# A recurrent recommendation kernel: the first 14 slots in another order, and the attention weights prepared in another way

## What is computed

```python
hs = _gru(hist, gru_W, gru_U, gru_b)
emb = jnp.concatenate([hs, news_b - hs, news_b, hs * news_b], axis=-1)
a = jax.nn.relu(jnp.einsum('bti,ij->btj', emb, att_W1) + att_b1)
a = jax.nn.relu(jnp.einsum('bti,ij->btj', a, att_W2) + att_b2)
ats = jax.nn.sigmoid(jnp.einsum('bti,ij->btj', a, att_W3) + att_b3)
...
def au_step(h, xs):
    xu_t, xr_t, xc_t, at_t = xs
    u = jax.nn.sigmoid(xu_t + h @ au_Uu)
    r = jax.nn.sigmoid(xr_t + h @ au_Ur)
    c = jnp.tanh(xc_t + r * (h @ au_Uc))
    u_ = at_t * u
    hn = (1.0 - u_) * h + u_ * c
    return (hn, None)
```

## Time and profile before

| | us |
|---|---|
| median of 3 runs | 1975.37 |
| lowest and highest | 1975.0, 1975.86 |
| the profiled execution | 1972.17 |
| its span, first to last instruction | 1970.3 |

### The profile page before, as it was taken

One profiled execution on the slowest core, in us unless ns is written; L12 is line 12 of the kernel. 1 busy time (PEld: TensorE's weight loads), 2 busy tenths in 40 slices (PEclk: granted clock), 3 DMA queues, 4 the chain that ended last, 5 costly groups with the idle time before them and its releaser, 6 DMA issues. The chain is left out here.

```text
span 1970.3 us, 29728 instructions
## 1 busy us (share of the span) xinstructions
PE 1934.8 (98%) x9190; PEld 861.8 (44%) x9190; DVE 1497.8 (76%) x2357; ACT 1452.0 (74%) x2466; POOL 1630.9 (83%) x1389
## 2 busy tenths in 40 slices
PE   8899999999999999999999999999999999999988
PEld 3344444444444444444444444444444444444433
DVE  5777777777777777777777777777777777777875
ACT  6677777777777777777777777777777777777754
POOL 6688888888888888888888888888888888888862
PEclk9999999999999999999999999999999999999999
DMA  3111111111111111111111111111111111111010
GB/s 122 54 44 71 49 48 66 51 51 50 70 48 48 70 48 53 48 70 48 48 70 50 51 48 69 48 48 70 53 48 48 69 48 50 69 52 48 33 44 22
DMA packets 37577, 108.15 MB, mean 55 GB/s; under 512 B 4329, under 2 KB 4585, under 8 KB 31153
## 3 DMA queue, kind: packets, MB, share of 16 engines
q1 hardware_dynamic: 37410, 107.60, 14.8%
q10 hardware_dynamic: 144, 0.26, 0.1%
HBM read 107.43 MB, written 0.42 MB: 55 GB/s over the span
## 5 line engine op out<-in xcount | busy, mean ns | idle before, releaser
L933 PE MATMUL ps<-h_hi,w_hi 128*128 128x512 f16 x1384 | 525.7, 380 | 19.7 <-DVE g L713 15.9
L934 PE MATMUL ps<-h_lo,w_hi 128*128 128x512 f16 x1384 | 524.8, 379 | 0.0
L935 PE MATMUL ps<-h_hi,w_lo 128*128 128x512 f16 x1384 | 524.8, 379 | 0.0
L306 POOL TENSOR_TENSOR hn_lo<-hn,hn_hi 128x512 f16<-128x512 f32 x200 | 232.4, 1162 | 182.2 <-ACT hn_hi L420 182.2
L300 POOL TENSOR_TENSOR hn<-h,news 128x512 f32<-128x512 f32 x200 | 256.1, 1281 | 74.1 <-DVE h L839 73.9
L566 ACT ACTIVATE ps<-gt,p_rest 128x512 f32<-128x512 f32 x196 | 135.3, 690 | 216.8 <-DVE gt L836 216.8
L370 POOL TENSOR_TENSOR gus<-gu,score 128x512 f32<-128x512 f32 x197 | 250.8, 1273 | 5.4 <-ACT gu L581 4.4
L319 POOL TENSOR_TENSOR x_lo<-x,x_hi 128x512 f16<-128x512 f32 x198 | 229.3, 1158 | 22.7 <-ACT x_hi L440 18.4
L363 POOL TENSOR_TENSOR g_lo<-g,g_hi 128x512 f16<-128x512 f32 x196 | 227.6, 1161 | 21.2 <-ACT g_hi L591 17.5
L827 DVE TENSOR_TENSOR gt<-gr,ps 128x512 f32<-128x512 f32 x196 | 135.0, 689 | 140.3 <-ACT gr L594 140.3
L377 POOL TENSOR_TENSOR d<-h,hc 128x512 f32<-128x512 f32 x186 | 236.7, 1273 | 0.4 <-ACT hc L587 0.4
(11 more groups left out here) (135 smaller groups left out, 3724.0 us busy)
## 6 DMA issues: line engine op xcount, KB each, us to landing
score<-score_rows SPq DMA_DIRECT2D x50, 1024.0 KB, 4.5
x<-in_xs SPq DMA_DIRECT2D x199, 256.0 KB, 3.0
news<-in_xs SPq DMA_DIRECT2D x4, 256.0 KB, 5.2
score_rows<-s_rows SPq DMA_DIRECT2D x50, 8.0 KB
p_rest<-in_pack_rest SPq DMA_DIRECT2D x1, 776.0 KB, 6.9
p_att<-in_pack_att SPq DMA_DIRECT2D x1, 322.0 KB, 5.4
x<-in_xs ACTq DMA_DIRECT2D x1, 256.0 KB, 4.0
p_gru<-in_pack_gru SPq DMA_DIRECT2D x1, 195.0 KB, 4.2
```

Source lines behind the costliest of these rows:

```text
L306: g.tensor_tensor(hn_lo[:, k, :], hn[:, k, :], hn_hi[:, k, :], ALU.subtract).then_inc(hnlo_ready, 1)
L933: m.matmul(ps[:, bank, :], w_hi[:, w, :], hi, start=start, stop=False)
L934: m.matmul(ps[:, bank, :], w_hi[:, w, :], lo, start=False, stop=False)
L935: return m.matmul(ps[:, bank, :], w_lo[:, w, :], hi, start=False, stop=stop)
```

## The change

- **Weights.** The pack of attention weights no longer holds the row of w3, and W1a, W1d and W2 stand side by side in it. W1a - W1b is written in place; the copy of W1d and both products with |w3| are gone, and one split of 320 columns takes the place of one of 384. |w3| is now the scale of the second layer's ReLU on ScalarE (an operand of one value a partition), and b2 is still multiplied by it.
- **Entry.** On VectorE the preparation is cut into parts that stand between the first states; the small ones (`prepare_att_2`) and the low parts of x of items 4 and 5, which GpSimd made before, stand ahead of the first attention sum. On ScalarE hn_hi(0), x_hi(4) and the c_news parts change places.
- **Slot 4.** On ScalarE hn_hi(3) goes behind the tanh and the sigmoid of the slot.
- **Slots 5, 9 and 13.** The first half of `attention_2` waits for two items less of a1_lo.
- **Slots 8 and 9.** The first score product goes from the end of slot 8 into its middle, and its sigmoid from the end of slot 8 to the place behind hn_hi of that slot.
- **Slots 10 to 13.** On TensorE the candidate product comes ahead of z, and the gated candidate input product (GXH) goes to the end. On VectorE step and state of g follow the difference at once. The splits of the gated weights stand one slot earlier.

```diff
-    SPLIT_X, SPLIT_G = LAG - 2, LAG + 2
+    SPLIT_X, SPLIT_G = LAG - 3, LAG + 1
...
             def early(low):
-                if low + 2 >= NC:
+                if low + 2 >= NC + 2:
+                    if low == NC:
+                        pool.wait_ge(xlo_ready, NC + 2)
                     input_low(low + 2, low + 3)
...
+            state_news_high(0, 1)
             reset_first(3)
             candidate_first(2)
-            second_high(0)
-            state_news_high(0, 1)
             state_high(1, 2)
             update_first(3)
+            second_high(0)
             candidate_first(3)
             act.wait_ge(att_landed, 16)
-            news_part(0)
             state_high(2, 3)
             state_news_high(1, 2)
+            news_part(0)
             news_part(1)
             second_high(1)
+            news_part(2)
             relu_1_high(0, 1)
-            news_part(2)
...
-                a.activation(ps[:, B_PAIR[p], :], ps[:, B_PAIR[p], :], ACT.Relu, bias=b_att2[:, 0:1]).then_inc(a2p_ready[p], NC)
+                a.activation(ps[:, B_PAIR[p], :], ps[:, B_PAIR[p], :], ACT.Relu, bias=b_att2[:, 0:1],
+                             scale=w3_col[:, 3:4]).then_inc(a2p_ready[p], NC)
...
-                if score_of(low - 1):
-                    score_rows_of(scored(low - 1), None)
                 if pairs_of(low - 1):
+                    if low - 1 == TILED:
+                        act.wait_ge(prep, 8)
...
                     news_part(3)
-                    act.wait_ge(a1_pe, 2)
-                    state_news_high(3, 4)
                     relu_1_high(1, 2)
                 else:
                     state_news_high(low - 1, low)
+                    if low == FIRST_SCORED:
+                        score_rows_of(NC, None)
                     relu_1_high(low - 2, low - 1)
...
                 if low == NC:
+                    act.wait_ge(a1_pe, 2)
+                    state_news_high(3, 4)
                     relu_1_high(2, 3)
...
                 if has(low - LAG - 1):
                     gated_difference(low - LAG - 1, low - LAG)
+                    gated_step(low - LAG - 1, low - LAG)
+                    gated_state(low - LAG - 1, low - LAG)
...
-                if has(low - LAG - 1):
-                    gated_step(low - LAG - 1, low - LAG)
                 attention_1_low(item, item + 1)
-                if has(low - LAG - 1):
-                    gated_state(low - LAG - 1, low - LAG)
...
             new_state_first(0)
-            prepare_att_terms()
-            prepare_att_blocks()
+            prepare_att_1()
             candidate_first(2)
             new_state_first(1)
-            split_att()
+            split_att_high()
             candidate_first(3)
             new_state_first(2)
+            split_att_low()
             new_state_first(3)
+            input_low(NC)
+            prepare_att_2()
+            input_low(NC + 1)
...
+                if low == FIRST_SCORED:
+                    pe.wait_ge(r_ready, low + 1)
+                    scores(NC)
                 if has(low - LAG):
-                    if low == LAG:
-                        pe.wait_ge(a1lo_ready, 2 * NC - 1)
-                    else:
-                        pe.wait_ge(g_ready, low - LAG)
-                    split_product(B_GXH, GW_C, *hg, start=True, stop=True).then_inc(gxh_pe, 1)
+                    candidate_part()
                     pe.wait_ge(gu_ready, low - LAG + 1)
...
-                pe.wait_ge(t1_ready, low + 1)
-                candidate_state(low - NC + 1, low - NC + 2)
-                if score_of(low):
+                if has(low - LAG):
+                    if low == LAG:
+                        pe.wait_ge(a1lo_ready, 2 * NC - 1)
+                    else:
+                        pe.wait_ge(g_ready, low - LAG)
+                    split_product(B_GXH, GW_C, *hg, start=True, stop=True).then_inc(gxh_pe, 1)
+                else:
+                    candidate_part()
+                if low > FIRST_SCORED and score_of(low):
+                    pe.wait_ge(r_ready, low + 1)
                     scores(scored(low))
                 if pairs_of(low):
-                    pe.wait_ge(a1lo_ready, low - 1)
+                    pe.wait_ge(a1lo_ready, low - 3)
                     pe.wait_ge(t2_ready, low + 1)
                     attention_2(0)
+                    pe.wait_ge(a1lo_ready, low - 1)
```

71 lines of the change are left out of this document (41 added, 30 removed).

## The result

The changed kernel takes 1956.47 us (median of 4 runs, 1956.07 to 1956.91) where the kernel before, run beside it, takes 1975.18 us (median of 4, 1971.69 to 1975.86). The ratio is 0.9907, with a 95% interval of 0.9895 to 0.9919. The forecast was 1958.9 us, so the kernel is faster, as said, and by 2.4 us more than the working gave. The profiled execution took 1956.07 us, 1954.2 us of it span; before it was 1972.17 and 1970.3 us. From profile to profile the span is 16.1 us shorter; the sum of the working was 16.5 us.

A forecast was written before the change was run, and what follows sets the result against it. TensorE was taken to bound the loop, leaving gains only in the first 115 us, at most 23.5 us. Terms summed to 16.5 us, taken off the 1975.37 us median: 1958.9 us, range 1954.5 to 1963.5 us.

The forecast's parts named there:

- Entry, +3.2 us: Kernel start: attention starts at 19.10 instead of 22.33 us, 3.2 us won, with a new 1.5 us wait.
- Slots 4 and 5, +2.4: Slot 5's candidate product loses its 1.88 us wait for t, 32.06 instead of 37.70 us: 2.4 us more won.
- the held instructions, -2.4: Small VectorE preparations before the first attention sum are held by GpSimd: 2.4 us lost, bounds 0 and 2.9.
- Rival (a): No holding on VectorE: 2.4 us more gained, 1956.4 us; chance 0.2.
- (b): All three VectorE instructions held, plus one more TensorE drop to 1.2 GHz (1.7 us): 1961.0 us; chance 0.25.
- (c): VectorE's instruction ring slower, 1 to 2 us a slot back in slots 11 to 14: 1963 to 1965 us; chance 0.08.
- (d): ReLU with a scale from memory much longer in 50 pairs; 1996.4 us at 1.0 us more each; chance 0.01.
- No slow stretch, +2.35: Slots 6 to 8 begin 8.0 us earlier without a 1.7 us slow stretch behind slot 5's wait: 2.35 us more won.
- The score, +2.6: Score sigmoid inside slot 8: the 2.66 us wait at slot 9's head shrinks to 0.3; 2.6 us won.
- slots 9 and 10, -0.65: Slot 9's second a1_lo comes some 0.7 us late and slot 10 loses 0.1: 0.65 us lost.
- Slots 11 to 13, +10.1: Waits for g (9.1 us) and a slow stretch (1.6) go, less 0.9 of new waits: 10.1 us won.
- Slot 14, -1.1: ScalarE starts slot 14 1.5 us further behind, making r late for the GR product: 1.1 us lost, once.

The follow-up runs named there:

- the kernel with nothing held ahead of the first sum: Changed kernel with the abs(w3) and b2 products in one-tensor-operand form, the w3 pair on ScalarE, x_lo(5) behind the first attention sum; 1954.28 us, ratio 0.9889.
- the kernel cut in three: Changed kernel with small preparations split: signs stay, products behind a1_lo(0), w3 pair in slot 5, x_lo(5) behind the first attention sum; 1955.84 us.
- the second run of the changed kernel: The changed kernel, unedited, measured once more beside the kernel before on another chip; 1956.33 us (1956.14 to 1957.9).

## Why the prediction was right, point by point

**Entry, +3.2 us.** Attention product 0 started at 19.15 us, predicted 19.10, for 22.33 before: 3.18 us. ScalarE's c_news(0) sets it, as the step says; it started at 18.36 us, predicted 18.35. Only the wait is 0.79 us and not 1.5: h of item 1 came later than I had it (a wait of 0.44 us at 14.11 us where none was to be), so the news products ended later, into the same end. I had given the in-place difference of the weights no hold, and it looks held as well:

```profile
11.40 1.39 DVE L666 TENSOR_TENSOR p_att<-p_att 128x128 f32<-128x128 f32 x1
```

GpSimd's hn stands beside it (11.38 us, 1.27 us long). The difference in the kernel before took 0.28 us, at 11.32 us and 0.03 us ahead of GpSimd's hn. No run tests this one apart. The 1.5 us of wait that the working had for c_news took the delay in.

**Slots 4 and 5, +2.4, and the held instructions, -2.4.** The candidate product of slot 5 was to start at 32.06 us with nothing held and at 34.46 with the price; it started at 34.27. In the kernel with nothing held ahead of the first sum it started at 32.28 us, although attention product 0 was 0.19 us later there: the price is shown at 2.2 us. TensorE pays it in three waits, 0.69 and 0.66 us for GpSimd's low halves and 0.30 us for t. It was composed otherwise than I said: the |w3| instruction in full (0.99 us), the subtraction behind it (1.15 us) and the first of the w3 pair (1.03 us), where the working had half of 1.0 us and one of 1.15 us, and nothing at x_lo(5), for which it had 0.75 us: that came when GpSimd had finished. The three holds are some 2.7 us longer than the same forms unheld (0.14, 0.15 and 0.23 us); the first sum needs attention product 0, whose last matmul ends at 20.60 us, so of its start at 23.05 us some 2.3 are the holds'. That 2.4 was so near is in part luck: one hold too small, one left out, one too many.

I had judged the |w3| instruction by the row of 0.14 us at 13.00 us and halved it. The rule of the Trainium skill (SBUF — State Buffer, "Who interferes with whom") would have been the better guide there: the |w3| instruction and the subtraction have two SBUF operands, and in the forms with one they ran in 0.15 to 0.21 us beside the same GpSimd rows. For the pair, which has one tensor operand, the same section says that a tensor_scalar can use both ports and then contends too; another page of the Trainium skill (VectorE: DVE Perf Modes, "Mode 2×_2P — use both read ports for one tensor") wants both operands in SBUF and the outermost dimension longer than one to be even, or odd and equal in source and destination; 32 columns are even, and one column has no such dimension. The rows of 1.03, 1.06 and 1.08 us for 32 columns and of 0.15 us for one agree; no run here changes the count alone, and none makes the pair on VectorE in another form.

**The rivals.** Rival (a) gives 1956.4 us, which is the measured median to 0.1 us, and it is wrong all the same: three instructions were held, and the kernel built to be (a) took 1954.28 us, 2.2 us less than the changed kernel, against the 2.4 of the working. The number alone would have picked it. In (b) the instructions were held more than I took as likely, but the 1.2 GHz stretch behind slot 5 did not come. (c) wanted 1 to 2 us a slot in slots 11 to 14, and there were 0.2 us. (d) needed 0.8 us more for each ReLU; it was 0.09.

**No slow stretch, +2.35.** Slot 6's hn product started at 39.90 instead of 45.59 us: 5.69, predicted 8.0 - 2.4 = 5.6. The granted clock is 1.00 throughout.

**The score, +2.6, and slots 9 and 10, -0.65.** Slot 9's hn product is 7.90 us earlier (64.50 to 56.60), 2.2 more than slot 6's, and slot 11's 7.24 us (77.73 to 70.49): -0.66. The wait is 0.35 us, predicted 0.3. Of the 2.6 us of the first 2.2 came. Put back, the score costs 1.7 us at slot 11 in the profiled run once its clock is taken out; the sum of the terms is 1.95 us.

**Slots 11 to 13, +10.1.** From hn product to hn product, slot 11 to slot 14: 31.20 us before, 21.27 now: 9.9. No wait for g. The bill I foresaw on VectorE came: the h instruction, the last of a slot there, starts at 69.61, 77.05, 84.58 and 91.71 us, 7.1 to 7.5 us apart, where TensorE's slots 11 to 13 take 6.5, 6.9 and 7.9 us. It stays all but hidden: one wait for t, of 0.23 us, at 86.31 us.

**Slot 14, -1.1.** The GR product is 15.97 us earlier (112.81 to 96.84) and the slot 17.17: -1.2, of which 0.89 is the wait for r.

The terms add to 16.0 us at the GR product, and 16.1 are left in the span.

**Why the median gained more.** I took the 16.5 us of one execution off a median. That execution had been a quick one, 3.2 us below the median of its kernel, and the profiled execution of the changed kernel is only 0.4 us below its own; that makes 2.8 us, and 0.4 us go the other way, for the gain of the spans is 16.1 us and not 16.5. Together this is the 2.4 us. The 27 runs of the kernel before on four chips have spans of 1970.3 to 1976.0 us and mean clocks of 0.997 down to 0.994. Half speed for x us lowers the mean by x/2 in 1970, so 0.997 is 5.9 and 0.995 is 9.9 us of lost clock (the clocks are given to 0.001, 2 us). The seven runs at 0.997 have a mean span of 1971.2 us, the twelve at 0.996 1973.4 and the seven at 0.995 1974.2: a good part of the scatter goes with the clock, but not all, for the longest of them, 1976.0 us, has 0.996. The changed kernel has waits of under 1 us from 6.1 us to slot 14 and a clock of 0.999 to 1.0: seven of its eight spans lie within 0.8 us. The step that was mis-sized is the last one, "I take it off the median": by the clocks, a median run of the kernel before had more stretches at 1.2 GHz than the profiled one. No median run of it was profiled, so where they stood is open.

**The scale operand.** The Trainium skill (ScalarE: Activation LUTs, "What ACT_TABLE_LOAD costs") gave 0.093 us for it; the means of 742 and 651 ns show 0.091. The working took it as hidden in the loop and as some 0.2 us in slot 14; the run without it shows 0.18 us there and 0.1 us in the span.

**The last score.** One term I had not seen when I wrote that the DMA is off the path. That holds for the first scores, but not for the last: at 1910 us it goes out by DMA and back to all partitions, and GpSimd's product waits for it. The chain that ended last, of the changed kernel:

```profile
1908.49 1.67 DMA score_rows<-s_rows
1910.17 4.18 DMA score<-score_rows
1914.48 1.28 POOL gus L370
```

Over the fifty transfers of that line the landing takes 4.2 to 4.9 us, so this path moves by up to 0.7 us from run to run. The g product behind it waited 1.46 us in the changed kernel, 1.77 in the one with free preparations and 2.00 in the one without scale, where the transfer took longer: that is where 0.3 and 0.5 us won earlier went.

## What to carry to other kernels

A wait that comes back in every slot of a pipeline's fill can be one half of a ring, as it was here by the rows: TensorE waits for g, so h comes late, so the next g does. Add up what each change takes off the wait, but no more than the wait itself: two changes of 1.95 and 1.8 us against a wait of 3.0 us don't bring 3.75. When an instruction is moved, its wait moves with it, and so does what holds it: the price of a place is the wait for the slow neighbour (1.48 us for GpSimd's sum), not the instruction's length. And an improvement read from one profile belongs to that execution; before it is taken off a median, compare the granted clocks of the runs.

## What was not expected of the hardware

An instruction of one column can cost as much as one of 512: 0.99 and 1.15 us for 128x1 outputs beside GpSimd's rows of 1.15 to 1.26 us, against 0.14 and 0.15 us for the same forms in the kernel before. And the hold depends on a hair of timing. The row of 0.14 us at 13.00 us started 0.03 us behind a row of GpSimd; the product for b2, also with two tensor operands, took 0.14 us at 20.93 us, 0.03 us ahead of GpSimd's next row. The held columns had started 0.13 us and more behind one. The two halves of the w3 pair, 1.03 and 0.24 us one behind the other, are the plain case: the second started when GpSimd had stopped, and where GpSimd went on, in the kernel that makes them in slot 5, they took 1.06 and 1.08 us.

TensorE's drop to 1.2 GHz is not a fixed consequence of a wait. The kernel with the score put back showed it behind a wait of 2.57 us, and by spans and clocks two of its four runs had it, at some 1.8 us each; a wait of 2.66 us in the same place of the kernel before was followed by none, and one of 1.88 us in the kernel cut in three was. At the last score, a wait of 1.99 us in the second run of the changed kernel was followed by one, and a wait of 2.00 us in the run without scale by none. What decides it stays open; no run here separates it.
